# Row maxima of two score products in one VectorE instruction, in a one-core attention and channel-mix layer

## The reference, cut to what matters

```
x = x + attn(layernorm(x))          # q, k with rope, softmax, v, then Wu and bu
x = x + channelmix(layernorm(x))    # sigmoid(R) * (relu(K)**2 @ W_v.T), token shift

dot = einsum('bhqd,bhkd->bhqk', q, k) / sqrt(16)
att = softmax(dot, axis=-1)
out = einsum('bhqk,bhkd->bhqd', att, v)
```

## Time and profile before

| | us |
|---|---|
| median of 3 runs | 2280.6 |
| lowest and highest | 2273.85, 2281.94 |
| the profiled execution | 2281.66 |
| its span | 2279.9 |
| TensorE busy | 2124.2 (93%) |
| VectorE busy | 2067.4 (91%) |
| ScalarE busy | 1645.7 (72%) |
| GpSimd busy | 1391.3 (61%) |

### The profile page before, as it was taken

The page is one execution under the profiler, slowest core; times in us unless marked ns, Lnnn a source line. Parts: engine busy times, 40 slices in busy tenths (PEclk is TensorE's granted clock), DMA queues, the critical chain, the costliest instruction groups (busy, mean ns, idle before and its releaser), DMA issues.

```text
span 2279.9 us, 39602 instructions
## 1 busy us (share of the span) xinstructions
PE 2124.2 (93%) x13084; PEld 1093.3 (48%) x13084; DVE 2067.4 (91%) x3982; ACT 1645.7 (72%) x3137; POOL 1391.3 (61%) x1184
## 2 busy tenths in 40 slices
PE   4999999999999999999999999999999999999995
PEld 3445444445454455444445444444545444545443
DVE  5899999999999999999999999999999999999862
ACT  2477777777777777777777777777777777777662
POOL 5347766666766666776566676566676566576334
PEclk8799999999999999999999999999999999999987
DMA  6544445544355554444564444554435555444410
GB/s 150 110 107 103 104 91 130 129 111 103 95 106 113 129 128 101 103 98 98 128 131 106 102 100 91 129 129 115 98 96 106 113 129 123 102 103 93 89 29 24
DMA packets 133466, 242.09 MB, mean 106 GB/s; under 512 B 24848, under 2 KB 79760, under 8 KB 120976
## 3 DMA queue, kind: packets, MB, share of 16 engines
q1 hardware_dynamic: 133264, 239.56, 46.7%
HBM read 136.71 MB, written 83.89 MB: 97 GB/s over the span
## 4 chain that ended last, share of the span: by engine, by line
PE 42%; DVE 32%; issue 10%; SPq 4%; POOL 4%; ACT 4%; DMA 3%; DVEq 0%; POOLq 0%; ACTq 0%
PE d_ps L955 17%; DVE mx L694 17%; PE st_ps L893 12%; PE pv_ps L925 8%; POOL f_lo L465 4%; PE s_ps L911 3%; DVE sums L718 3%; SPq L318 2%; DVE ve L759 2%; PE d_ps L949 2%; SPq L329 2%; ACT probs L653 2%; DVE stats L748 2%; DVE attn L730 2%; DMA q_st<-mparts 1%
## 5 line engine op out<-in xcount | busy, mean ns | idle before, releaser
L653 ACT ACTIVATE probs<-st_ps 128x512 f32<-128x512 f32 x2048 | 1154.8, 597 | 505.2 <-PE st_ps L893 483.6
L694 DVE TENSOR_REDUCE mx<-s_ps 128x1 f32<-128x512 f32 x2048 | 1324.4, 676 | 117.4 <-PE s_ps L911 114.1
L893 PE MATMUL st_ps<-q_st,k_st 50*128 50x512 f32 x2048 | 804.4, 459 | 45.7 <-ACT probs L653 29.8
L911 PE MATMUL s_ps<-k_st,q_st 48*128 48x512 f32 x2048 | 815.8, 464 | 30.8 <-DVE mx L694 20.8
L893 PEld LDWEIGHTS st_ps<-q_st,k_st 50*128 50x128 f32 x2048 | 324.1, 186 | 664.3 <-ACT probs L653 450.5
L925 PE MATMUL pv_ps<-probs,v_ext 128*32 128x512 f32 x4096 | 549.7, 609 | 0.2 <-DVE sums L718 0.2
L473 POOL TENSOR_TENSOR rs<-ve,mhalf 128x2 f32<-128x2 f32 x128 | 90.3, 706 | 444.7 <-DVE mean L760 444.7
L911 PEld LDWEIGHTS s_ps<-k_st,q_st 48*128 48x128 f32 x2048 | 327.2, 186 | 61.7 <-DVE mx L694 50.8
L465 POOL TENSOR_TENSOR f_lo<-yn,f_hi 128x512 fp32r<-128x512 f32 x128 | 175.2, 1379 | 107.8 <-ACT f_hi L618 107.8
L435 POOL TENSOR_TENSOR parts<-parts 128x1024 fp32r<-128x1024 f32 x62 | 148.1, 2389 | 60.4 <-ACT parts L583 60.4
L723 DVE TENSOR_TENSOR sums<-sums,inv 128x256 f32<-128x256 f32 x128 | 164.0, 1281 | 4.4
(11 more groups left out here) (116 smaller groups left out, 3959.4 us busy)
## 6 DMA issues: line engine op xcount, KB each, us to landing
parts_scratch<-parts SPq DMA_DIRECT2D x64, 1024.0 KB, 4.5
q_st<-parts_scratch SPq DMA_DIRECT2D x128, 256.0 KB, 5.5
k_st<-parts_scratch SPq DMA_DIRECT2D x128, 256.0 KB, 6.6
xn<-in_L_attn_x_dram SPq DMA_DIRECT2D x32, 512.0 KB, 9.2
q_st<-parts_scratch SPq DMA_DIRECT2D x128, 128.0 KB, 7.0
k_st<-parts_scratch SPq DMA_DIRECT2D x128, 128.0 KB, 7.4
attnT<-attn SPq DMA_DIRECT2D x512, 32.0 KB, 2.0
y<-in_L_attn_x_dram SPq DMA_DIRECT2D x32, 512.0 KB, 6.5
```

The lines of the kernel that those rows point to most:

```text
L653: nc.scalar.activation(probs[:, u % SLOTS, j, :], st_ps[:, n % 2, :], ACT.Exp, scale=float(D) ** -0.5).then_inc(exp_done, 1)
L694: nc.vector.tensor_reduce(mx[:, col:col + 1], s_ps[:, ring_bank(n), :], AX.X, ALU.max).then_inc(max_done, 1)
L893: nc.tensor.matmul(st_ps[:, n % 2, :], k_st[par][row:row + SROWS + MROWS, slot, c * P:(c + 1) * P], q_st[par][row:row + SROWS + MROWS, slo ...
L911: nc.tensor.matmul(s_ps[:, ring_bank(n), :], q_st[at][row:row + SROWS, slot, qc * P:(qc + 1) * P], k_st[at][row:row + SROWS, slot, :], sta ...
```

## The change

In `row_max`, the products are looked at in pairs: n even and n+1, which are steps 0 and 1, or 2 and 3, of a unit. Where the two lie in neighbouring banks (distance 1 either way), nothing is issued at the even step, and at the odd step one TENSOR_REDUCE reads both banks as 128 x 2 x 512 and writes two columns of `mx`, and raises `max_done` by 2. It waits for the second product. Where they lie in banks 2 and 0, each keeps its own instruction. The last pair of a batch lies in banks 2 and 1 and is read with a negative step. The extras stay at their steps, so that one that was hung on an even step now comes ahead of the maxima of both. The two halves of the 16 columns of a group in `mx` change places, and `move_max` reads them from there; its DMAs are as many and as large.

```
                             sp.dma_start(dst[row:row + 1, 2 * g:2 * g + 2, :].bitcast(F32)
                                          .rearrange("p h (c t) -> p (h c) t", c=TC),
-                                         mparts[half * 2 * TC:(half + 1) * 2 * TC, m, :].bitcast(F32)).then_inc(mrow_in, 16)
+                                         mparts[(1 - half) * 2 * TC:(2 - half) * 2 * TC, m, :].bitcast(F32)).then_inc(mrow_in, 16)
...
                 def row_max(u, qc):
                     s, n = row_max_at(b, u, qc)
-                    if s.active():
-                        half, pair, chunk = max_place(n)
-                        col = GH * TC * (pair // 2) + 2 * TC * half + TC * (pair % 2) + chunk
-                        dve.wait_ge(s_ready, s.count(SCORES, n + 1))
-                        nc.vector.tensor_reduce(mx[:, col:col + 1], s_ps[:, ring_bank(n), :], AX.X, ALU.max).then_inc(max_done, 1)
+                    if not s.active():
+                        return
+                    near, far = ring_bank(n - qc % 2), ring_bank(n - qc % 2 + 1)
+                    joined = abs(far - near) == 1
+                    if joined and qc % 2 == 0:
+                        return
+                    m = n - 1 if joined else n
+                    half, pair, chunk = max_place(m)
+                    col = GH * TC * (pair // 2) + 2 * TC * (1 - half) + TC * (pair % 2) + chunk
+                    dve.wait_ge(s_ready, s.count(SCORES, n + 1))
+                    if joined:
+                        bank = s_ps[:, near, :]
+                        both = bass.AP(bank.tensor, bank.offset, [bank.ap[0], [(far - near) * T, 2], [1, T]])
+                        nc.vector.tensor_reduce(mx[:, col:col + 2 * TC + 1:2 * TC], both, AX.X, ALU.max).then_inc(max_done, 2)
+                    else:
+                        nc.vector.tensor_reduce(mx[:, col:col + 1], s_ps[:, near if qc % 2 == 0 else far, :],
+                                                AX.X, ALU.max).then_inc(max_done, 1)
```

## The result

| | us |
|---|---|
| before, median | 2280.0 |
| after, median | 2406.0 |
| lowest and highest after | 2404.1, 2407.0 |
| ratio, with its 95% interval | 1.0552 (1.0533 to 1.0570) |
| the profiled execution: span before, after | 2279.9, 2405.3 |

The change costs 126 us, or 5.5%. The direction was forecast, the size was not: 32 us were forecast, and the time lies far above the stated range.

A forecast was written before the change was run, and what follows sets the result against it. Neither TensorE nor VectorE alone was taken as the bound; they hand it over within every batch. 0.31 + 0.59 + 0.19 - 0.07 = 1.02 us, times 31 batches, adds 32 us: median 2312, own range 2295 to 2330, whole range 2262 to 2342.

The forecast's parts named there:

- two joined in a row, counted: Second joined maximum waits for a product needing a bank the first still reads; 12 a batch, delay counted at three.
- The prices: Joined maximum 1.21 us; bank release to score 0.05 us; score start to maximum start 0.57 us.
- a slot saved: VectorE: a joined maximum occupies 1.13 us against 1.20 for two singles, saving 0.07 us, 47 us in all.
- the rival of the costlier instruction: Joined instruction saves nothing on record (1.28 us); five ring waits each 0.14 us later, 2334 us; chance 0.18.
- The three places that were worked out: Units (10), (13) and (0), where TensorE has no idle time before: +0.31, +0.59 and +0.19 us a batch.
- Most of them are hidden. At (3), (4) and (14) VectorE waits for the products anyway.: Of 12 neighbouring joined pairs a batch, those outside (10), (13) and (0) were given no cost.
- the price of nothing for the 0.53 us at (2,1): TensorE held up to 0.53 us more at (2,1), but the delay ends at (4,0), which waits for DMAs.
- The ring's stop is covered: Rival: the VectorE saving shows; 2257 us with half the joined pairs on the path, 2233 with all; faster: 0.15.
- no difference: Rival: TensorE's work and DMA and GpSimd waits bound the batch, or saving and stops cancel; 2281 us; chance 0.19.
- What would show it: Signs: 704 maxima at 1.21 us, VectorE 45 us less busy, five late scores, longer units, batch period 68.2 from 67.2 us.
- The sign that was put for the sum: TensorE's scores idle for mx by 60 us or more where it was 21.

## Why the prediction was wrong, point by point

The table takes the mean length of each unit over 28 inner batches (from the start of its first score_T to that of the next unit's), after less before; a batch takes 67.60 us before and 71.42 after.

| units | forecast | measured | how the forecast saw them |
|---|---|---|---|
| 10 and 11 | +0.31 | +0.66 | two joined in a row, counted |
| 13 and 14 | +0.59 | +0.60 | two joined in a row, counted |
| 0 and 1 | +0.19 | +0.07 | two joined in a row, counted |
| 2 and 3 | 0 | +1.11 | hidden; measured: the clock above all |
| 4, 5 and 6, 7, 8 and 9, 12, 15 | 0 | +1.39 | hidden or not looked at; measured: short waits at the ring |
| all | +1.02 (less 0.07 saved) | +3.82 | |

By cause, the 3.82 us are about 0.96 of clock (18 of 28 batches at 1.5), 0.44 of unit 10's longer form (13 more of 28 at 0.95), and 2.4 of waits at the ring with what follows them.

**The prices held.** A joined maximum was put at 1.21 us and takes 1.217; a slot saved was put at 0.07, 47 us in all, and VectorE is busy 42 us less. The ring's release (0.05) and the start of the next maximum (0.57) are as read the earlier trace rows. Two-row reading adds nothing, so the rival of the costlier instruction was not it.

**The three places that were worked out** gave 1.33 us where 1.09 had been put, but 0.44 of it is the longer form of unit 10, which the forecast did not have. The wait at (10,3) was right, 0.64 us where it had 0.63. Those at (13,3) and (14,1) are smaller, 0.29 and 0.12 where it had 0.42 and 0.17, and (0,3) hardly waits. That (13) and (14) agree to a hundredth is luck: what the waits lack is made up by the 0.11 us of slower restart behind each, which was left out of the sum. Nor is it the row of two joined ones that makes (10,3) and (13,3) wait: with the pairs of steps 0 and 1 alone they wait 0.65 and 0.45 us.

**The step that failed is "Most of them are hidden. At (3), (4) and (14) VectorE waits for the products anyway."** The argument is that where TensorE sets the pace, a later maximum costs nothing. It holds for VectorE's own start, not for the release. In such a place the maximum starts as soon as it can, and still the bank is held to 0.54 + 1.23 us after the odd score's start, while TensorE is back at the bank after 1.67. The numbers for this stood in the prediction, 0.57 and 1.21; 1.67 stands in the timeline of the kernel before. They were never put side by side for a pair in steps 2 and 3 followed by step 1. Only neighbours that were both joined were looked at, 12 of the 22 pairs; the run with steps 2 and 3 alone has none of them and loses 85 us.

**The second step that failed** is the price of nothing for the 0.53 us at (2,1). The length was right, 1.07 to 1.54 us of wait on average, and that it "ends there" is nearly right for the wait itself: with this pair alone, batches that keep their clock, with unit 10 in its short form, take 67.44 us where they took 67.17, so 0.27 of the 0.53 gets through, and in the changed kernel nothing is gained by taking the pair out (70.61 us with it, 70.66 without, where the score of (2,3) waits 0.45 us instead). But TensorE's clock fell behind the wait in more than half of the batches: unit 2 takes 7.27 us there and 5.74 in the others. In the kernel before it is full in every inner batch, and I took it as given. That term is 18 x 1.5 = 27 us in the inner batches of the changed kernel, where the two runs on that one pair gave 17 and 29. The first two batches, where the clock is at half for longer stretches before and after, are longer by 13 us together, 5 more than two inner ones.

**The rivals.** "The ring's stop is covered" is refuted with it, and so is "no difference". The advice cited from the Trainium skill's "Perfetto Trace Analysis", section "Optimizing Scalar/DVE Operations", is to break instructions up where VectorE is not saturated but causes bubbles on other engines. VectorE is busy for 84% of the span after, and the measurements bear the advice out: two singles with two releases against one joined, 2298 and 2406 us. Its 125 ns of overhead an instruction on PSUM is not borne out: 704 instructions fewer took 42 us off VectorE, 60 ns each.

**What would show it** was partly right: 704 at 1.21, 45 us less on VectorE, the places (10,3), (13,3), (14,1), (2,1) late, but (0,3) not. Unit 13 is longer by 0.39 us (0.4 was put) and unit 10 by 0.91 (0.6); the period grew by 3.82 us, not 1.0. (The 67.2 that was put for it before is a batch with the short form of unit 10; the mean is 67.60.) The sign that was put for the sum, the score's idle time for mx at 60 us or more, was read in the wrong row. The page's row for the products has 46.0 us for mx, where it was 20.8, but most of the wait stands before the loads, 50.8 us before and 138.9 after, and the forecast looked only at the first.

## What to carry to other kernels

An instruction that takes two buffers of a ring at once holds the first for the length of both. So before joining, take for each pair the time in which the producer comes round to the first buffer, and set against it start, full length and release; 0.15 us too little in a dozen places costs more than the instruction saves. Do it at the places where the producer sets the pace, too: there the consumer has room to start, but the ring has none to release. And where a longer wait falls on TensorE, count a possible drop of its clock behind it, and not the wait alone. When small gains are compared, look first for a place that has two lengths in one and the same trace, as unit 10 here: how often it takes the longer one can outweigh what was changed.

## What the runs showed of the hardware

- A TENSOR_REDUCE over 128 x 2 x 512 in two neighbouring PSUM banks takes 1.217 us, one over 128 x 512 0.676, one over 128 x 2 x 256 0.686. The second row costs its elements and no more, with the step positive or, once a batch, negative.
- Where the score of (2,1) started 1.5 to 1.6 us behind its score_T, 1.06 to 1.10 of them idle, a stretch of 3.4 us at a granted 1.2 instead of 2.4 GHz followed in 16 of 26 batches after, and in 7 of 27 in the run with that pair alone. Where it started 1.07 us behind, 0.58 of them idle, before the change, in none of 28.
- A 128x2 TENSOR_SCALAR on VectorE that takes 0.15 us took 1.08 in 9 of 28 inner batches before and in 22 after, and ended 0.02 to 0.03 us behind a 128x512 TENSOR_TENSOR that GpSimd had under way.
